# Turning attention probabilities in 32x32 blocks on VectorE, and setting key halves side by side by transfers

## What is computed

```python
DEPTH, HEADS, DIM_HEAD, WINDOW = 6, 16, 64, 32
def local_attention(q, k, v):            # windows of 32 queries
    bk2, bv2 = look(bk), look(bv)        # keys and values: the window before, and its own (64)
    sim = einsum('bhwie,bhwje->bhwij', bq, bk2) * QK_SCALE
    sim = where(mask, -finfo.max, sim)
    attn = softmax(sim, -1)
    return einsum('bhwij,bhwje->bhwie', attn, bv2)
def attn_layer(x, ...):                  # q, k: unit norm, scale, rotary
    q, k, v = split(x @ Wqkv, 3, -1)
    ...
    return local_attention(q, k, v) @ Wo
for i in range(DEPTH):
    x = attn_layer(shift_tokens(x), ...) + x
    x = ffn_layer(shift_tokens(x), ...) + x   # LayerNorm, a * gelu(gate), W2
```

## Time and profile before

| | us |
|---|---|
| median of 3 runs (3801.88 to 3802.43) | 3801.89 |
| span of the profiled execution | 3803.9 |
| PE busy | 3594.4 |
| DVE busy | 3264.6 |
| POOL busy | 2752.8 |
| ACT busy | 2374.7 |

### The profile page before, as it was taken

The page is one execution under the profiler, slowest core; times in us unless marked ns, Lnnn a source line. Parts: engine busy times, 40 slices in busy tenths (PEclk is TensorE's granted clock), DMA queues, the critical chain, the costliest instruction groups (busy, mean ns, idle before and its releaser), DMA issues. The chain is left out here.

```text
span 3803.9 us, 157044 instructions
## 1 busy us (share of the span) xinstructions
PE 3594.4 (94%) x61680; PEld 2336.5 (61%) x61680; DVE 3264.6 (86%) x11515; ACT 2374.7 (62%) x4331; POOL 2752.8 (72%) x2632
## 2 busy tenths in 40 slices
PE   6799999999999999997699689999999999999998
PEld 4466666666666666662466456666666666666665
DVE  6898888888888889865799798889898888889885
ACT  2567667666766767663422257667676766767665
POOL 1788888878888888852144288888887888888883
PEclk9899999999999999998799699999999999999999
DMA  1232323323322332220000132233233232332222
GB/s 46 77 85 71 81 73 78 87 67 74 85 73 69 85 75 66 66 65 16 0 1 6 29 81 72 74 87 78 71 80 76 71 81 74 83 78 68 66 69 57
DMA packets 170286, 250.95 MB, mean 66 GB/s; under 512 B 36544, under 2 KB 67264, under 8 KB 169408
## 3 DMA queue, kind: packets, MB, share of 16 engines
q1 hardware_dynamic: 169536, 240.72, 25.4%
HBM read 38.21 MB, written 1.05 MB: 10 GB/s over the span
## 5 line engine op out<-in xcount | busy, mean ns | idle before, releaser
L592 PE MATMUL stack_work<-stack_w_qkv,stack_xs 128*128 128x512 f32 x2304 | 1148.0, 604 | 34.4 <-ACT stack_sq L883 17.8
L1244 POOL TENSOR_TENSOR stack_roped<-stack_rot_c,stack_rot_s 128x512 f32<-128x512 f32 x768 | 984.6, 1304 | 148.5 <-DVE stack_rot_s L1052 148.2
L1254 POOL TENSOR_TENSOR stack_roped<-stack_roped,stack_rnorm 128x512 f32<-128x512 f32 x768 | 794.6, 1045 | 188.7 <-DVE stack_rnorm L1084 188.7
L883 ACT ACTIVATE stack_sq<-stack_work 128x512 f32<-128x512 f32 x768 | 443.3, 594 | 485.6 <-DVE stack_rot_s L1052 485.1
L1050 DVE TENSOR_TENSOR stack_rot_c<-stack_work,rot_tables 128x512 f32<-128x512 f32 x768 | 526.8, 686 | 130.4 <-PE stack_work L592 112.9
L592 PEld LDWEIGHTS stack_work<-stack_w_qkv,stack_xs 128*128 128x128 f32 x2304 | 400.5, 191 | 384.4 <-issue 323.9
L1270 POOL TENSOR_TENSOR stack_s_m<-stack_s_m,stack_inv 128x512 f32<-128x512 f32 x384 | 400.8, 1044 | 276.4 <-DVE stack_inv L1113 276.1
L1052 DVE TENSOR_TENSOR stack_rot_s<-stack_work,rot_tables 128x512 f32<-128x512 f32 x768 | 521.6, 679 | 0.0
L1061 DVE TENSOR_REDUCE stack_ssq<-stack_sq 128x8 f32<-128x512 f32 x768 | 496.7, 667 | 6.0 <-issue 4.4
L641 PEld LDWEIGHTS stack_bank_o<-stack_p_t,stack_v_w 64*64 64x64 f32 x24576 | 394.5, 135 | 171.9 <-issue 147.4
L600 PE MATMUL stack_work<-ident,stack_roped 128*128 128x128 f32 x3072 | 452.2, 280 | 8.3 <-issue 5.8
(11 more groups left out here) (257 smaller groups left out, 5269.0 us busy)
## 6 DMA issues: line engine op xcount, KB each, us to landing
stack_v_w<-stack_v_nat SPq DMA_DIRECT2D x1152, 128.0 KB
stack_v_w<-stack_v_nat SPq DMA_DIRECT2D x768, 64.0 KB
stack_w_qkv<-table_ffn_qkv SPq DMA_DIRECT2D x192, 96.0 KB, 2.3
stack_w_o<-table_ffn_wo SPq DMA_DIRECT2D x12, 512.0 KB, 4.2
stack_w<-table_ffn_w SPq DMA_DIRECT2D x12, 384.0 KB, 3.3
stack_w<-table_ffn_w SPq DMA_DIRECT2D x12, 192.0 KB, 3.1
x_outer<-L_attn_a_X SPq DMA_DIRECT2D x4, 256.0 KB, 6.9
ret_xpos<-table_xpos SPq DMA_DIRECT2D x1, 1024.0 KB, 6.2
```

Of the source, the lines that this page charges most:

```text
L592: pe.matmul(bank[:, :], xs[:, T, :], w_qkv[:, g.half, col:col + 512], start=True, stop=True).then_inc(done["proj_" + c], 1)
L883: act.activation(sq[:, i % 2, :], work[(BANK["p_" + c][T] + g.row) % 4][:, :], ACT.Square).then_inc(done["squared_" + c], 1)
L1244: pool.tensor_tensor(roped[:, i, T % 2, :], rot_c[:, i % 2, :], rot_s[:, i % 2, :], ALU.add).then_inc(done["roped_" + c], 1)
L1254: pool.tensor_tensor(r, r, rnorm[:, T % 2, i, :].unsqueeze(2).broadcast_to([P, 8, HD]), ALU.mult).then_inc(done["united_" + c], 1)
```

## The change

The probabilities are turned by DVE instead of PE: `turn_probs` is now a block transpose of 32x32 blocks, from `s_m` to `p_turned`, one for each key half j (a parity of heads) and tile. It leaves the two halves of a window's 64 keys (the window before, and its own) on the same 32 partitions; eight transfers a tile, `spread_probs`, set them on neighbouring 32 partitions in `p_pairs`. For windows 1 and 3 the values lie as needed in `v_nat` itself; for windows 0 and 2 four transfers a tile fill `v_even`. `v_nat` is four tiles deep instead of two. The two weighing calls of a tile follow each other, and one copy takes both out.

```diff
-        xs = sb("xs", [P, 4, P])
-        v_nat = sb("v_nat", [P, 2, 2, 8, HD])
-        v_w = sb("v_w", [P, 2, 4, 8, HD])
+        v_nat = sb("v_nat", [P, 4, 2, 8, HD])
+        v_even = sb("v_even", [P, 2, 2, 8, HD])
-        p_t = sb("p_t", [P, 2, 4, P])
+        p_turned = sb("p_turned", [P, 2, 2, PAIRS, WINDOW])
+        p_pairs = sb("p_pairs", [P, 2, 2, 2, PAIRS, WINDOW])
...
-            "p_q1": (1, 1, 0, 3),
+            "p_k0": (1, 2, 1, 2),
...
-            run_slots(16 * (DEPTH - 1), 4 * (DEPTH - 1), DEPTH - 1, 1, 16 + 12)
+            run_slots(16 * (DEPTH - 1), 4 * (DEPTH - 1), DEPTH - 1, 1, 16 + 16)
...
-                for gp in range(2):
-                    half = 64 * gp
-                    sp.dma_start(v_w[half + 32:half + 64, b, 0, :, :], v_nat[0:32, b, gp, :, :]).then_inc(v_in[b], 16)
-                    sp.dma_start(v_w[half:half + 32, b, 0, :, :], v_nat[96:P, 1 - b, gp, :, :]).then_inc(v_in[b], 16)
-                    for n4 in range(1, 4):
-                        sp.dma_start(v_w[half:half + 64, b, n4, :, :], v_nat[32 * (n4 - 1):32 * (n4 + 1), b, gp, :, :]
-                                     ).then_inc(v_in[b], 16)
+                for to, window, before in ((0, 0, 0), (64, 2, 0), (32, 3, 1), (96, 1, 0)):
+                    sp.dma_start(v_even[to:to + WINDOW, b, :, :, :],
+                                 v_nat[WINDOW * window:WINDOW * (window + 1), (n - before) % 4, :, :, :]
+                                 ).then_inc(v_in[b], 16)
+
+            def spread_probs(layer, n):
...
+                sp.wait_ge(done["turned_p0"], tile + (tile0 + 1))
...
+                sp.wait_ge(done["turned_p1"], tile + (tile0 + 1))
...
+                    sp.wait_ge(done["weighed1"], tile + (tile0 - 1))
...
+                for window in range(4):
+                    rows = slice(WINDOW * window, WINDOW * (window + 1))
+                    other = WINDOW * (window - 1 if window % 2 else window + 1)
+                    sp.dma_start(p_pairs[rows, b, window % 2, :, :, :], p_turned[rows, 1, :, :, :]).then_inc(p_in[b], 16)
+                    sp.dma_start(p_pairs[other:other + WINDOW, b, window % 2, :, :, :], p_turned[rows, 0, :, :, :]
+                                 ).then_inc(p_in[b], 16)
...
-            def turn_probs(t, T, g, j, bank):
...
-                wait(pe, f"prob{j}", t)
-                for n in range(4):
-                    last = pe.transpose(bank[:, P * n:P * (n + 1)], s_m[:, T % 2, j, 2 * n:2 * n + 2, :], ident[:, :])
-                last.then_inc(done[f"pe_pt{j}"], 1)
...
-                wait(pe, f"pt_set{j}", t)
...
-                for half in range(2):
-                    for n in range(4):
-                        for odd in range(2):
-                            for gp in range(2):
-                                m, at = 2 * half + odd, P * half + WINDOW * n
-                                last = pe.matmul(bank_o[HD * odd:HD * (odd + 1), gp, at:at + WINDOW],
-                                                 v_w[64 * gp:64 * gp + 64, T % 2, n, 2 * m + j, :],
-                                                 p_t[64 * gp:64 * gp + 64, j, m, WINDOW * n:WINDOW * (n + 1)],
-                                                 start=True, stop=True)
+                if j == 0:
+                    pe.wait_ge(v_in[T % 2], (2 * g.number + (tile0 // 2 + T // 2 + 1)) * 64)
...
+                    pe.wait_ge(p_in[T % 2], (2 * g.number + (tile0 // 2 + T // 2 + 1)) * 128)
...
+                for gp in range(2):
+                    for half in range(2):
+                        for odd_window in range(2):
+                            at = WINDOW * (2 * (4 * j + 2 * gp + half) + odd_window)
+                            for two in range(2):
+                                rows = slice(64 * two, 64 * two + 64)
+                                values = v_nat[rows, T, gp, :, :] if odd_window else v_even[rows, T % 2, gp, :, :]
+                                for odd in range(2):
+                                    m = 2 * half + odd
+                                    last = pe.matmul(bank_o[HD * odd:HD * (odd + 1), two, at:at + WINDOW],
+                                                     values[:, 2 * m + j, :], p_pairs[rows, T % 2, odd_window, j, 2 * m + gp, :],
+                                                     start=True, stop=True)
...
-            def probs_out(t, T, g, j):
...
+            def turn_probs(t, T, g, j):
...
+                wait(dve, f"prob{j}", t)
+                if live(t - 1):
+                    dve.wait_ge(p_in[(T - 1) % 2], (2 * g.number + (tile0 // 2 + (T - 1) // 2 + 1)) * 128)
+                dve.transpose(p_turned[:, :, j, :, :].rearrange("p f h q -> p h f q"), s_m[:, T % 2, j, :, :]
+                              ).then_inc(done[f"turned_p{j}"], 1)
...
-            def stage(t, T, g):
...
-                pool.tensor_copy(xs[:, T, :], xst[:, g.row, P * T:P * (T + 1)]).then_inc(done["staged"], 1)
```

More of the change, by code:

```diff
@@ L583, in _, with project, turn @@
         def _(pe):
[L584 removed]
+            def project(t, T, g, c):
                 if not live(t):
                     return
[L587 to L590 removed]
+                if c == FIRST_IN and T == 0:
+                    wait_x(pe, g.number - BATCH)
+                    apart(pe, t)
+                    pe.wait_ge(qkv_in, (g.layer + (layer0 + 1)) * 256)
                 col = 512 * PARTS[c]
[L592 to L595 removed]
+                pe.matmul(work[(BANK["p_" + c][T] + g.row) % 4][:, :], xst[:, g.row, P * T:P * (T + 1)],
+                          w_qkv[:, g.half, col:col + 512], start=True, stop=True).then_inc(done["proj_" + c], 1)
+            def turn(t, T, g, c):
                 if not live(t):
@@ L598, in turn @@
                 wait(pe, "united_" + c, t)
+                bank = work[(BANK["t_" + c][T] + g.row) % 4]
                 for n in range(4):
@@ L668, in variance, with up @@
                 wait_group(pe, "center_sq", g)
-                pe.matmul(bank[:, :], mean_m[:, :], c_sq[:, :], start=True, stop=True).then_inc(done["pe_var"], 1)
-            def up(g, kind, k, bank):
+                pe.matmul(work[(BANK["va"] + g.row) % 4][:, :], mean_m[:, :], c_sq[:, :], start=True, stop=True
+                          ).then_inc(done["pe_var"], 1)
+            def up(g, kind, k):
                 if not live_group(g):
@@ new lines, in slot @@
+                    turn(*at(6), "k1")
+                    wait_group(pe, "hid0", G - 4)
+                    turn(*at(6), "q1")
+                    wait(pe, "squared_q0", N - 4)
+                    project(*at(7), "v1")
+                    wait_group(pe, "hid1", G - 4)
+                    project(*at(4), "k1")
+                    wait(pe, "masked0", N - 7)
+                    wait(pe, "masked1", N - 7)
+                    scores(*at(6), 0)
+                    scores(*at(6), 1)
+                    wait(pe, "kept_k1", N - 6)
```

729 lines of the change are left out of this document (414 added, 315 removed).

## The result

The changed kernel takes **3652.18 us** (median of four runs, 3644.31 to 3657.49), the kernel before on the same chip 3802.16 us. The ratio is 0.9597, with a 95% interval of 0.9584 to 0.9611: 4.0% faster, some 150 us, where 57 were forecast.

A forecast was written before the change was run, and what follows sets the result against it. PE was taken as bound, DVE as next: 192 tiles going from 16.46 to 16.06 us give -77 us, ramps +20, so -57 and 3745 us; likeliest case 3710 to 3785, whole range 3660 to 3880.

The forecast's parts named there:

- These steps remain three a tile: DVE's 32-element steps, 751, 711 and 533 ns with waits for POOL inside, were left unchanged in DVE's work.
- a rival, at a chance of 0.12: PE stays the bound as 32-element steps fall into POOL's pauses and DVE waits less: 3640 us, half way 3690; chance 0.12.
- DVE's idle time, put at 0.7%: DVE as next bound idles the share seen with PE as bound, so 15.95 us of work gives 16.06 a tile.
- The order was priced at nothing: The engines' new lists were given no cost or gain a tile, only two more slots of ramp a stack.
- ramps: Filling and draining the pipeline takes two more slots a stack: +10 us a stack, +20 us in all, bounds 0 and +33.
- PE's relief: PE loses 0.92 us a tile of turning and 0.14 of weighing, falling from 16.46 to 15.40 us.
- The transposes: Two 128x512 block transposes a tile on DVE at 0.64 us each, bounds 0.60 and 1.3, raise DVE to 15.95 us.
- the products' order: In PE's weighing, neighbouring products now use the same array rows and different columns; priced at nothing.
- ACT, POOL's and SP's covers: ACT and POOL lose copies, which buys nothing; SP's transfer issues, 7.5 to 8.7 us a tile of 16, stay hidden.
- no gain: DVE and PE wait for each other; half the idle time stays, 16.4 to 16.5 us a tile, 3790 to 3825; chance 0.15.
- DVE busy over 98%: Sign that the forecast is right: DVE's busy share in the steady windows after the change.
- PE is the bound: Before the change PE, busy 99.3% of the steady middle at 16.46 us a tile, limits the kernel; DVE is next.

The follow-up runs named there:

- new order with nearly the old loads: Changed kernel with DVE turning one head pair of eight per call and PE turning the k0 and q0 pieces twice: 3721.44 us, ratio 0.9777.
- the kernel with PE alone lightened: Kernel before with three of eight head pairs left out of the output projection, 0.70 us a tile less on PE: 3732.76 us, ratio 0.9814.
- the kernel with both edits: Kernel before with each tile's two sums of probabilities formed twice on DVE and three of eight head pairs left out of PE's output projection: 3879.76 us, ratio 1.02.

## Why the prediction was wrong

**The step that failed** is "These steps remain three a tile, and POOL stays as dense as before [...] I leave them as they are". POOL did stay as dense (84.5% of the window, before 81.6%), but the steps meet it less often and nearer to its end, and the three lost 0.87 us a tile. Of what the four steps lost together, 2154 to 1380 ns, about two thirds (to 1653) came with the new order at nearly the old loads. The prediction had this mechanism as the first half of a rival, at a chance of 0.12, and took 3690 for half of the waits lost; more than half went. A second term of the same sum failed the other way: DVE's idle time, put at 0.7% (0.11 us a tile), was 3.5% (0.55). With 15.07 + 0.55 the tile is 15.62 us instead of 16.06.

**The order was priced at nothing** beyond its ramps, and that is the larger lesson. Four corners, each against before on its own chip: old order and old loads, 0; old order with nearly the new loads, +74 us; new order with nearly the old loads, -86; both new, -150 and -162 in two measurements. The two single changes add up to -12, so most of the gain is in having both. The rule "the next bound is DVE's work plus 0.7%" foretold 16.06 us a tile; the old order under these loads takes 16.97 and 16.87. The new order at the new loads is worth 74 + 155, about 230 us, or near 190 if the 0.36 us more that the change takes off PE are paid at the rate of the kernel with PE alone lightened (73 us for 0.70; with DVE loaded, the same 0.70 gave 7). So two errors of opposite sign stood in the sum: with these stand-ins, moving the work to DVE costs time in the old order, and at the new loads the order gains more than the whole result. One limit stays: the stand-in for the transposes is a second sum, and it stands ahead of the sum that the inverse and POOL's scaling wait for, while the transposes come at the end of that chain. How much of the +74 is this place, and not the order, no run tells.

**Point by point.** PE's relief was right: from the busy 16.35 us, less 0.92 and 0.14, it gives 15.29, and 15.23 was measured. (The forecast took it from the period of 16.46 instead and wrote 15.40, which counts 0.11 us of idle time as work.) The transposes were right: 0.64 us taken, 0.69 long, and the next DVE start comes 0.62 later (1011.61 to 1012.23, below), without waiting for POOL. The price of nothing for the products' order was right. ACT, POOL's and SP's covers held, and so did the transfers' (3.6 us of PE's waiting in all). The ramps were right, +24 us for +20. The rival "no gain" was mispriced: half of the 1.79 us of idle time on top of DVE's 15.95 is 16.85 us a tile, not 16.4 to 16.5, and 16.87 to 16.97 is what the old order shows at these loads. "DVE busy over 98%" was wrong (96.5%), and so was PE's 95 to 96% (97.5%).

```profile
1011.61 0.70 DVE L1151 STREAM_TRANSPOSE stack_p_turned<-stack_s_m 128x512 f32<-128x512 f32 x1
1012.23 0.16 DVE L1110 TENSOR_TENSOR stack_u_n<-stack_u_n,stack_ssq 128x32 f32<-128x32 f32 x1
```

**The start was wrong too.** "PE is the bound" rested on 99.3% busy. Taking 0.70 us a tile from PE in that kernel gave 73 of 134 us, and taking steps from DVE gave 38 though PE had 0.7% of idle time. A PE that is busy all the time had time in it that wasn't work: in the kernel with both edits it shows 482.54 us over 500 / 16.97 = 29.5 tiles, 16.4 us a tile, with 0.70 us less to do than before's 16.35. The Trainium skill, "Perfetto Trace Analysis", section on identifying performance opportunities, says that matmul busy time is no good measure of how close TensorE is to its limit, and to look at the rate of arithmetic and the share of weight loads; that share is 66% here before (345.40 of 526.70 us) and 64% after. The runs agree on the first point: at 99.3% busy, 0.70 us less work a tile gave 73 of 134 us.

**Open** stays which of the order's changes does it: the larger lags between a tile's stages, the one weighing of both halves, or the places of POOL's operations. For the steps alone the places can be read from the traces, over 450 to 1450 us and by slot of four. Before, the second step stood right behind a rotation in all four slots and met POOL's addition each time (295, 1153, 807 and 520 ns), and the first step met POOL's subtraction in three (921 to 942 ns). After, the second step is behind a rotation in two slots (288 and 673 ns) and behind a transpose in two (146 and 617), and the first has 601, 423, 321 and 171 ns. Two local shifts of DVE's list moved the waits among the steps and cost at most 18 us; larger pieces of the order were not tried one by one.

## What to carry to other kernels

Where several engines run fixed lists and little is idle, as here with PE at 99%, DVE at 89% and POOL at 82% of the time, the lists are a term of the sum: price a move of work and a new order apart, and test the new order with the old loads before crediting the move. A wait that hides inside an instruction's duration (same operation, same size, 0.17 or 0.75 us) is no work and can go when the other engine's list changes; list such waits first and bound what losing them would give. A stand-in for moved work should also stand at the moved work's place in the list. Taking such steps away altogether, here two small ones, one of them given to ACT with its time to spare, was worth another 60 us, while giving one to the engine that they wait for cost 50.

## What the runs showed of the hardware that was not expected

- A 32-element step of DVE that starts while POOL is in an instruction ends just after that instruction does. Of 1901 steps that met a POOL instruction with over 150 ns to go (all seventeen traces, 450 to 1450 us), 1892 ended 33 to 56 ns after it; the other 9 had started within 33 ns of POOL's start and took 142 to 176 ns. With POOL idle a step takes 0.14 to 0.19 us. It holds for the step with one SBUF input as well (L1103, ends some 37 ns behind POOL).
- It is not a matter of size. The 128x512 product for `x_c`, with two SBUF inputs, started while POOL was in an instruction all 16 times after the change (450 to 1450 us) and took 1.40 us, 0.55 of them behind POOL's end. The 128x512 block transpose doesn't wait (687 and 699 ns), nor do sums over 512 elements (665 to 676 ns in all kernels) or the 128x8 reciprocal (190 ns with POOL running, 194 without).
- PE's busy time a tile isn't constant for the same products: it was 16.35 us before, and 16.4 with 0.70 us of products removed and DVE loaded, in a tile of 16.97.
- Work on an engine has no one price: 0.60 us added to DVE cost 72% of itself, 0.9 taken off gave 24%, and 1.25 added in the old order cost 80 of 240 us.
